# Attention with routed experts on one core: row sorting between the maxima, a first group begun on half its queries, a lead built over five groups, fills in pieces

## The chip, the cores and the metric

One core of a Trainium2 chip runs the whole program in one launch. The metric is the device time of a launch in microseconds (us). TensorE is called PE here, VectorE DVE, ScalarE ACT, GpSimd POOL, and SP is the engine that issues most DMAs.

## What is computed

The input is 4 x 1024 rows of 256, in float32. The rows are normalised; attention with 16 heads of 16 (with relative positions in a window of 4 to each side) and a mixture of 8 experts, 2 per row, both read the normalised rows, and the sum of both and the input is the output:

```python
xn = _layernorm(x, axis=-1)
x = x + _L0_attn_ref(xn, Wq, bq, Wk, bk, Wv, bv, Wo, bo, emb_rel_k, emb_rel_v) + _L0_ffn_ref(xn, gate_w, gate_b, w1, w3, w2)
# attention: softmax(q k^T + relative logits) v + relative weights x rel_v, then Wo
# experts:
logits = x @ gate_w + gate_b
top_w, top_idx = jax.lax.top_k(softmax(logits), 2)      # weights made to sum to 1
h = silu(x @ w1[e]) * (x @ w3[e]);  out = sum over the two e of (h @ w2[e]) * top_w
```

## The kernel before, in words

**Stages.** `build` runs `constants`, `norm_and_project`, `attention`, `finish_and_experts` and `combine`, each in a block of its own. A block starts when every engine has ended the one before it, so it also waits for the DMAs that SP waits for at its end.

**`norm_and_project`** takes 8 chunks of 512 rows (loop `chunks`). VectorE normalises the next chunk (L293) from `xt`, which SP loads (L200) after it has stored the one before (`put_xn`); PE projects q, k, v; ScalarE and VectorE split q and k into two float16 parts (L400, L334), which SP stores as `q_parts` and `k_parts` (L208). VectorE's L334 comes once a chunk. After chunk 3, `load_stack` (L91) issues 18 DMAs of 128 KB on SP's queue: the stacks of q and k for the first pass of groups 0 and 1 and for the second pass of group 0. All of them are waited for at the end of the block.

**`route`** (row sorting) is added to the same block after the chunks. From the gate logits VectorE finds each row's two experts, the row's place in a list sorted by expert, and the expert of each slot of 256 rows: some 60 small instructions of at most 128 x 312 elements, each waiting for the one before (L1021 to L1077). In between are one exponential on ScalarE (L1082) and two matmuls that count rows (L1088, L1089), read from PSUM by VectorE. Nine POOL instructions make its constants at the start of the block.

**`attention`** handles 16 groups of 4 heads of one batch entry. Each group has two passes. The first pass finds each query's maximum: 32 tiles of 128 queries x 1024 keys; PE makes a tile in two halves (`pass1`, L723) into one of two PSUM buffers of 1024 (`s1`), and VectorE takes its maximum (L838). Three small VectorE instructions (L842 to L845, "parts") split the 32 maxima into two float16 numbers; PE transposes them (L768), ScalarE copies them to `mt` (L904), and SP writes them as two rows into the query stack (L604), so that the second pass subtracts them in the matmul. The second pass has 64 slots: PE makes 128 keys x 512 queries (`pass2`, L733 and L737) into one of three buffers, ScalarE takes the exponential (L915), and PE sums the values (`values`, L750).

PE's order is written out in `group`: in slot n of a group's second pass it also issues first-pass matmuls of the next group, with a constant lead of 20 halves (`LEAD`); the first-pass and second-pass matmuls use different rows of the array. Group 0 has nobody ahead of it: its whole first pass runs alone, then in its own 64 slots PE issues 84 first-pass halves. The maxima of group g+1 are finished in slot 55 of group g. All of PE's instructions are in one order, so a wait in a first-pass matmul holds the second pass too.

**POOL in `attention`** makes the products of the window (32 tiles, three per group; `products` L652, `fold` L661 and L665, `add_to_band` L672, from SBUF to SBUF). Tile t waits until the parts of group t // 3 are made (`mparts_ok`). When all 32 are done it sends the rows to their slots: 64 indirect DMAs (`send`, L691), from rows loaded by `load_rows` (L677; the first two loads are issued at the start of the block).

**SP in `attention`** (`step`) writes the maxima's rows, then loads the stacks of coming groups. Between the steps it fills `slot_rows` with zeros (13 DMAs of 780 KB in steps 0 and 1) and, between steps 9 and 10, `expert_sums` with one DMA of 4224 KB (L634).

**`finish_and_experts`** runs the experts' slots; its VectorE line L1515 (two tensors from SBUF) and L1537 (one from PSUM, one from SBUF) and its POOL lines L1268 and L1270 (products from SBUF) are used by the prediction as examples. The change doesn't touch this stage.

Of the kernel before, what the change touches and what calls it, by code (L numbers as in the profile page):

```python
# [12 lines left out]
P = 128  # L13
# [6 lines left out]
CH = 512  # L20
# [81 lines left out]
def norm_and_project(nc, c, dr, x, Wq, bq, Wk, bk, Wv, bv, rel_k, gate_w, gate_b, band, dst, meta, spare, table, iota_e, slot_expert, size, w1, w3, wsum, stacks):  # L102

    with ExitStack() as ctx:
# [34 lines left out]
        logits = sb("logits", [P, NT, X])  # L139
# [34 lines left out]
        with nc.Block() as block:  # L174
            @block.sync
            def _(sp):
# [33 lines left out]
                def chunk(n, u, b):  # L210
# [28 lines left out]
                for u in range(2):  # L239
                    sp.wait_ge(stacks["in1"][u], 16 * 2 * len(Q_PARTS))  # L240
                sp.wait_ge(stacks["in2"][0], 16 * 2 * len(Q_PARTS))
# [260 lines left out]
            route(nc, block, ctx, logits, rel_out, pT, dst, meta, spare, table, iota_e, slot_expert)  # L502


def attention(nc, c, dr, stacks, band, bmax, neg, oa, dst, meta, spare):
# [5 lines left out]
    XS = 2 * TB * HG  # L511
    FOLDS = 4
    MLEAD = 9
    LEAD = 20
    MT = (LEAD - MLEAD + 1) // 2
    X1 = TB * HG
    B1, B2, BP = 2, 3, 4
    with ExitStack() as ctx:
# [57 lines left out]

        def far_pieces(tile, half):
# [8 lines left out]

        with nc.Block() as block:
            @block.sync
            def _(sp):
# [9 lines left out]

                def maximum(g, u):  # L600

                    sp.wait_ge(mt_ok, g + 1)
                    for j in range(MROWS):
                        sp.dma_start(qs[SIDE + j:SIDE + j + 1, u].rearrange("o h (i t) -> o (h i) t", t=P),  # L604
                                     mt[j * HG * TB:(j + 1) * HG * TB, :]).then_inc(m_in, 16)
# [16 lines left out]

# [5 lines left out]
                for z in range(N_ZERO // 2, N_ZERO):  # L628
                    sp.dma_start(zeros[z], zero[:].broadcast_to([P, 6, XE])).then_inc(zero_out, 16)
                for r in range(NB - 2):  # L630
                    for v in range(4):
                        step(4 * r + 2 + v, r + 1, v, v % 2)
                sums = dr["moe"].rearrange("(n p) e -> p n e", p=P)
                sp.dma_start(sums, zero[:, :, 0:E].broadcast_to([P, NT + 1, E])).then_inc(sums_out, 16)  # L634
# [5 lines left out]
                sp.wait_ge(sums_out, 16)  # L640

            @block.gpsimd
            def _(pool):
                nc.gpsimd.memset(zero[:], 0.0).then_inc(zero_ok, 1)
# [51 lines left out]
                load_rows(0)  # L696
                load_rows(1)
                for t in range(2):
                    load_window(pool, dr, t, qw[:, t, :], kw[:, t, :], win_in[t])
                for t in range(NT):  # L700

                    pool.wait_ge(mparts_ok, t // 3 + 1)
# [4 lines left out]
                    add_to_band(t, t % 2)  # L707
                for t in range(NT):
# [5 lines left out]
            def _(pe):  # L714
                def pass1(g, u, n):

                    n, half = n // 2, n % 2
                    h, i, buf = n // TB, n % TB, n % B1
                    if half == 0:
                        if n == MT or n == 0 and isinstance(g, int) and g == 1:  # L720
                            after(pe, mt_ok, g)
                        after(pe, mx_ok, g * X1 + n - B1 + 1)
# [40 lines left out]
                def maximum_rows(g, ahead=True):  # L763

                    pe.wait_ge(mparts_ok, g + 1)
                    if ahead:
                        pe.wait_ge(mx_ok, (g + 1) * X1 + MT - 1)
# [951 lines left out]
```

## Time and profile before

| | us |
|---|---|
| median of 3 runs | 1891.03 |
| lowest and highest | 1886.86 and 1902.19 |
| the profiled execution | 1900.86 |
| its span, first to last instruction | 1899.1 |
| PE / VectorE / ScalarE / POOL busy | 1699.1 / 1451.0 / 1097.8 / 811.7 |
| mean granted clock of PE (1 is 2.4 GHz) | 0.926 |

The stages of the profiled execution: the projection to 187.6, the row sorting to 207.0, group 0's first pass to 250.1, the 16 groups' second passes to 1031, the experts to some 1850, and the output. Durations in the rows are those of this one execution; busy time can hide waits inside an engine's pipeline, so the rows of waits and the starts of instructions are read beside it.

### The profile page before, as it was taken

What the parts mean: (1) busy time and instruction counts of PE and PEld (TensorE: products, weight loads), DVE (VectorE), ACT (ScalarE), POOL (GpSimd) and SP (SyncE); (2) the same over time, 40 slices, a digit from 0 to 9 for tenths busy, and PEclk for the clock granted to TensorE, in tenths of its full rate; (3) what the DMA queues carried; (4) which work ended last, traced back from release to release, by engine and by line L of the source; (5) the groups of instructions that cost most, each with busy time, mean ns of one, the idle gap of its engine ahead of it and who ended that gap; (6) DMA issues with size and microseconds to landing.
All of it is one profiled execution on the core that took longest, in us unless ns stands there. A gap on an engine that the chain in (4) does not pass through costs nothing. (4 is left out here: it accounts for less than half of the span.)

```text
span 1899.1 us, 35153 instructions
## 1 busy us (share of the span) xinstructions
PE 1699.1 (89%) x13691; PEld 1021.4 (54%) x13691; DVE 1451.0 (76%) x2569; ACT 1097.8 (58%) x2122; POOL 811.7 (43%) x587
## 2 busy tenths in 40 slices
PE   5968589999999997689996799999999999999991
PEld 3746023333333331223332687888788878888881
DVE  4535988988888984378852798999899989997652
ACT  3646047888888884368884544554455445545540
POOL 3000077778888886600000344544454445442110
PEclk9988579999999997689995899999999999999996
DMA  5999246975556655523102777777777777765745
GB/s 177 372 305 359 103 106 178 249 201 129 129 143 150 150 139 189 160 47 59 30 2 87 248 237 228 233 254 234 231 231 253 235 231 230 253 210 180 210 137 185
DMA packets 199846, 355.25 MB, mean 187 GB/s; under 512 B 17008, under 2 KB 145920, under 8 KB 191488
## 3 DMA queue, kind: packets, MB, share of 16 engines
q1 hardware_dynamic: 163360, 225.19, 40.6%
q0 software_dynamic: 27744, 106.84, 18.6%
q10 hardware_dynamic: 8576, 20.97, 3.0%
q8 instruction: 108, 1.77, 0.4%
q14 instruction: 58, 0.48, 0.1%
HBM read 281.47 MB, written 71.22 MB: 186 GB/s over the span
## 5 line engine op out<-in xcount | busy, mean ns | idle before, releaser
L838 DVE CUSTOM_DVE_ANT_0 t_seen<-t_s,hide 128x1024 bf16<-128x1024 f32 x512 | 608.4, 1222 | 135.1 <-PE t_s L723 105.8
L915 ACT ACTIVATE t_pr<-t_s 128x512 f32<-128x512 f32 x1024 | 558.8, 603 | 177.2 <-PE t_s L737 105.5
L723 PE MATMUL t_s<-ks,qs 48*128 48x512 f16 x1024 | 372.5, 414 | 36.2 <-PEq L174 12.6
L733 PE MATMUL t_s<-qs,ks 50*128 50x512 f16 x1024 | 363.7, 400 | 31.0 <-issue 17.6
L1444 ACT ACTIVATE e_sg<-e_pa,e_down 128x256 f32<-128x256 f32 x312 | 148.0, 474 | 396.9 <-PE e_pa L1319 387.5
L750 PE MATMUL t_po<-t_pr,t_vx 128*32 128x256 f32 x4096 | 344.7, 410 | 0.0
L1515 DVE SCALAR_TENSOR_TENSOR e_wl<-e_ws,e_up,e_wh 128x512 f16<-128x512 f32 x312 | 318.6, 1033 | 13.3
L1328 PE MATMUL e_py<-e_w2s,e_hT 128*128 128x256 f32 x1248 | 322.9, 381 | 0.0
L1256 POOL DMA_INDIRECT expert_sums<-e_y,e_token x78 | 139.7, 1791 | 294.0 <-DMA expert_sums<-e_y,e_token 205.0
L1319 PE MATMUL e_pa<-e_xh,e_wh 128*128 128x256 f16 x1248 | 239.8, 274 | 25.6 <-DVE e_xl L1507 18.6
L733 PEld LDWEIGHTS t_s<-qs,ks 50*128 50x128 f16 x1024 | 89.1, 94 | 285.6 <-ACT t_pr L915 173.9
L1319 PE MATMUL e_pa<-e_xl,e_wh 128*128 128x256 f16 x1248 | 239.2, 274 | 0.0
L1319 PE MATMUL e_pa<-e_xh,e_wl 128*128 128x256 f16 x1248 | 239.1, 273 | 0.0
L1328 PEld LDWEIGHTS e_py<-e_w2s,e_hT 128*128 128x128 f32 x1248 | 212.8, 190 | 22.0
L1537 DVE SCALAR_TENSOR_TENSOR e_hT<-e_pa,e_down,e_sg 128x256 f32<-128x256 f32 x312 | 145.8, 467 | 94.9 <-ACT e_sg L1444 94.9
L1405 ACT ACTIVATE e_wh<-e_ws,e_up 128x512 f16<-128x512 f32 x312 | 217.4, 711 | 0.0
L652 POOL TENSOR_TENSOR t_kw<-t_kw,t_qw 128x2304 f32<-128x2304 f32 x32 | 162.8, 5088 | 99.6 <-issue 62.2
L1319 PEld LDWEIGHTS e_pa<-e_xh,e_wh 128*128 128x128 f16 x1248 | 117.2, 98 | 83.4 <-DVE e_xl L1507 31.4
L661 POOL TENSOR_TENSOR t_kw<-t_kw 128x1152 f32<-128x1152 f32 (+2 forms) x96 | 149.9, 1562 | 7.5
L737 PEld LDWEIGHTS t_s<-far,eye 64*128 64x128 bf16 x1152 | 108.6, 98 | 69.5 <-issue 13.0
L737 PE MATMUL t_s<-far,eye 64*128 64x72 bf16 (+2 forms) x1152 | 141.6, 194 | 0.0
L723 PEld LDWEIGHTS t_s<-ks,qs 48*128 48x128 f16 x1024 | 84.6, 95 | 102.9 <-DVE t_mx L838 73.6
(231 smaller groups left out, 1936.4 us busy)
## 6 DMA issues: line engine op xcount, KB each, us to landing
e_ws<-in_L_ffn_w_dram SPq DMA_DIRECT2D x78, 1024.0 KB, 5.0
e_w2s<-in_L_ffn_w_dram SPq DMA_DIRECT2D x39, 1024.0 KB
t_kw<-k_rows POOLq DMA_DIRECT2D x32, 1152.0 KB, 8.9
e_vs<-v_rows POOLq DMA_DIRECT2D x32, 1152.0 KB, 6.0
a_wone<-in_L_ffn_w_dram ACTq DMA_DIRECT2D x16, 1024.0 KB, 10.3
qs<-q_parts SPq DMA_DIRECT2D x96, 128.0 KB, 4.0
ks<-k_parts SPq DMA_DIRECT2D x96, 128.0 KB, 6.4
slot_rows<-t_zero SPq DMA_DIRECT2D x13, 780.0 KB, 14.6
```

What stands on the lines that cost most here:

```text
L652: nc.gpsimd.tensor_tensor(held, held, qw[:, u:u + 1, :].broadcast_to([P, NM, E]), ALU.mult).then_inc(mul_ok, 1)
L661: nc.gpsimd.tensor_tensor(terms[:, :, 0:w], terms[:, :, 0:w], terms[:, :, w:2 * w], ALU.add).then_inc(fold_ok, 1)
L723: last = nc.tensor.matmul(s1[:, buf, half * CH:(half + 1) * CH], qs[lows, u, h, i * P:(i + 1) * P], ks[lows, u, h, half * CH:(half + 1) * ...
L733: last = nc.tensor.matmul(s2[:, bank, :], ks[highs, u, h, i * P:(i + 1) * P], qs[highs, u, h, half * CH:(half + 1) * CH], start=True, stop ...
L737: last = nc.tensor.matmul(s2[:, bank, a:a + m], c["eye"][SIDE:P, r, :], c["far"][SIDE:P, r, j:j + m], start=False, stop=(x == len(far) - 1 ...
L750: last = nc.tensor.matmul(po[h * VW:(h + 1) * VW, cols], vx[:, u, i, h * VW:(h + 1) * VW], pr[:, k % BP, h, cols], start=(i == 0 and part ...
L838: nc.vector.tensor_tensor_reduce(out=seen[:, buf, :], in0=s1[:, buf, :], in1=c["hide"][:, (TB - 1 - i) * P:(TB - 1 - i) * P + L], scale=1. ...
L915: nc.scalar.activation(pr[:, k % BP, n % HG], s2[:, turn(u, n)], ACT.Exp, scale=SPREAD ** -2).then_inc(exp_ok, 1)
L1319: last = nc.tensor.matmul(pa[:, f % PA, j, :], w[:, u, j, k, f * P:(f + 1) * P], x[:, u, k, :], start=(i == 0), stop=(i == len(parts) - 1))
L1328: last = nc.tensor.matmul(py[:, i, 0:E], hT[:, f, i * P:(i + 1) * P], w2s[:, u, f, :], start=(f == 0), stop=(f == FC - 1))
L1405: nc.scalar.activation(wh[:, u, m, k, cols], ws[:, m, k, cols], ACT.Copy, scale=up[:, m, bass.ds(s, 1)]).then_inc(wh_ok, 1)
L1515: nc.vector.scalar_tensor_tensor(out=wl[:, u, m, k, cols], in0=ws[:, m, k, cols], scalar=up[:, m, bass.ds(s, 1)], in1=wh[:, u, m, k, cols] ...
```

## The change

Five edits.

- **Row sorting** becomes a class `Route`. Its POOL constants are made at the start of the attention block. VectorE's instructions are yielded one by one by a generator; `maxima` takes the next one after maxima 1, 5, 9, ..., 29 of each group from 1 on (`ROUTE_EVERY`), so 8 per group and 61 places (some left empty) in groups 1 to 8. The exponential stands behind slot 56 of group 1 on ScalarE, the two counts are made by PE with the transpose of group 3's maxima, and ScalarE copies them to SBUF. The order and shapes of the instructions stay. POOL's two first `load_rows` come after the products, behind a wait for the sorted places.
- **First group.** PE makes 18 tiles of group 0 (now in an order that takes the first 4 query tiles of every head first), then half of the maxima go to the stack: 8 small DMAs in place of 2; the second pass starts on the first half of the queries. The other 14 tiles come in slots 0 to 21, their maxima follow at slot 22 by another 8 DMAs, and PE waits for them at slot 32. Group 1's first pass comes in slots 22 to 58.
- **Lead.** The lead of the first pass is 12 halves in group 1, then 14, 16, 18 and 20; the last groups are as before. ScalarE's `mt` copy and the buffers of the transposes follow from the lead.
- **Stack loads.** After chunk 6 only 6 loads are issued (first pass of group 0); the other 12 come first on SP's queue in the attention block.
- **Fills.** `expert_sums` is filled by 7 DMAs of up to 640 KB, one after each of steps 2 to 8.

The diff, cut to its core:

```diff
-                    if n == 3:
+                    if n == NC - 2:
                         for p in range(PARTS):
                             sp.wait_ge(st_part[p], 16 * 2 * KC * 2)
                         load_stack(sp, dr, stacks, 0, 0, 0, stacks["in1"])
-                        load_stack(sp, dr, stacks, 0, 0, STACK, stacks["in2"])
-                        load_stack(sp, dr, stacks, 1, 1, 0, stacks["in1"])
...
-            route(nc, block, ctx, logits, rel_out, pT, dst, meta, spare, table, iota_e, slot_expert)
+class Route:
...
+    def choose(self, dve):
...
+            self.steps += 1
+            ins.then_inc(self.chain, 1)
...
+            then(nc.vector.tensor_tensor(self.eq[:], src[:], over_x(m[:, k, :]), ALU.is_equal))
+            yield
...
-    LEAD = 20
-    MT = (LEAD - MLEAD + 1) // 2
-    X1 = TB * HG
+    LEADS = [36 - XS] + [min(12 + 2 * (g - 1), 20) for g in range(1, NG)]
+    TURN0, TURN1 = 22, 59
+    HALF = X1 // 2
+    FIRST_ROWS = 2 * MROWS * HG
+    GATES_AT, COUNT_AT = 1, 3
+    ROUTE_EVERY = 4
+    SUMS = 5
...
+        def first_passed(g, n):
+
+            if g == 0 and n < TURN0:
+                return XS + LEADS[0] + -(-(2 - LEADS[0]) * (n + 1) // TURN0)
+            if g == 0:
+                return XS + 2 + min(-(-XS * (n + 1 - TURN0) // (TURN1 - TURN0)),
+                                    XS + max(0, -(-(LEADS[1] - 2) * (n + 1 - TURN1) // (XS - TURN1))))
+            more = LEADS[min(g + 1, NG - 1)]
+            return min(NG * XS, XS * (g + 1) + LEADS[g] + -(-(XS + more - LEADS[g]) * (n + 1) // XS))
...
+                def half_maximum(u, half):
+
+                    sp.wait_ge(mt_ok, half + 1)
+                    for j in range(MROWS):
+                        for h in range(HG):
+                            row = (j * HG + h) * TB + half * CT
+                            sp.dma_start(qs[SIDE + j:SIDE + j + 1, u, h, half * CH:(half + 1) * CH].rearrange("o (i t) -> o i t", t=P),
+                                         mt[row:row + CT, :]).then_inc(m_in, 16)
...
+                load_stack(sp, dr, stacks, 0, 0, STACK, in2)
+                load_stack(sp, dr, stacks, 1, 1, 0, in1)
                 load_values(0, 0, 0)
-                maximum(0, 0)
+                half_maximum(0, 0)
                 load2(1, 0, 1, 1)
...
                 load1(2, 0)
-
+                half_maximum(0, 1)
                 step(0, 0, 2, 0)
...
-                sp.dma_start(sums, zero[:, :, 0:E].broadcast_to([P, NT + 1, E])).then_inc(sums_out, 16)
+                        piece = slice((4 * r + v) * SUMS, min((4 * r + v + 1) * SUMS, NT + 1))
+                        if piece.start < NT + 1:
+                            sp.dma_start(sums[:, piece], zero[:, :, 0:E].broadcast_to(
+                                [P, piece.stop - piece.start, E])).then_inc(sums_out, 16)
...
-                load_rows(0)
-                load_rows(1)
...
-                    pool.wait_ge(mparts_ok, t // 3 + 1)
+                    pool.wait_ge(mparts_ok, t // 3 + 2)
...
+                pool.wait_ge(route.dst_ok, 1)
+                load_rows(0)
+                load_rows(1)
...
                     for n in range(X1):
...
+                        if g == 0 and n == HALF - 1:
+                            dve.wait_ge(mx_ok, HALF)
+                            parts(slice(0, CT), 0)
+                        if g and n % ROUTE_EVERY == 1:
+                            after(dve, route.chain, route.steps)
+                            next(routing, None)
```

## Rows read from the trace of the kernel before

**Rows 1.** windows by stage: engine columns are busy us (instructions), then clock, DMA share, GB/s.
```profile
187.60:207.00 19.40, 0.58 (x2) 0.14 (x2) 17.00 (x56) 0.23 (x1) 0.01 (x1) 0.50 0.22 76
309.64:699.30 389.66, 386.24 (x4187) 140.62 (x4185) 347.33 (x604) 326.17 (x621) 318.18 (x215) 1.00 0.66 167
699.30:846.96 147.66, 110.08 (x933) 34.73 (x930) 78.41 (x135) 73.25 (x138) 76.55 (x82) 0.76 0.48 138
```

**Rows 2.** timeline of VectorE and of SP in chunks 4 to 6 (start, us, instruction).
```profile
112.58 2.48 DVE L334 SCALAR_TENSOR_TENSOR a_part<-a_qkT,size,a_part 128x1024 f16<-128x1024 f32 x2 [3.17 <-DMA k_parts<-a_part]
...
136.25 1.08 DVE L277 BATCH_NORM_STATS2 a_st<-a_xt 128x6 f32<-128x256 f32 x3 [19.79 <-DMA a_xt<-_attn_hidden_states_dram]
...
146.13 2.48 DVE L334 SCALAR_TENSOR_TENSOR a_part<-a_qkT,size,a_part 128x1024 f16<-128x1024 f32 x2 [1.82 <-DMA k_parts<-a_part]
...
164.23 2.47 DVE L334 SCALAR_TENSOR_TENSOR a_part<-a_qkT,size,a_part 128x1024 f16<-128x1024 f32 x2
...
114.37 0.51 SPq L200 DMA_DIRECT2D a_xt<-_attn_hidden_states_dram  x1
```

**Rows 3.** start of the attention block, and a window of the DMA engines before it.
```profile
192.00:194.00 2.00, 0.13 (x1) 0.14 (x2) 1.68 (x6) 0.14 (x1) 0.00 (x0) 0.50 0.01 3
...
207.00 0.37 SPq L594 DMA_DIRECT2D t_vx<-vx_rows  x1
```

**Rows 4.** timeline around the first second pass, and a window of group 0.
```profile
208.20 1.22 DVE L838 CUSTOM_DVE_ANT_0 t_seen<-t_s,hide 128x1024 bf16<-128x1024 f32 x1 [1.01 <-PE t_s L723]
...
246.01 0.18 DVE L842 TENSOR_SCALAR t_mparts<-t_mx 128x32 f16<-128x32 f32 x1
...
247.33 1.26 SPq L604 DMA_DIRECT2D qs<-t_mt  x2
...
250.09 0.58 PE L733 MATMUL t_s<-qs,ks 50*128 50x512 f16 x1 [3.08 <-DMA qs<-t_mt]
...
250.06:275.40 25.34, 24.25 (x181) 7.82 (x181) 21.37 (x35) 14.79 (x26) 23.93 (x17) 0.69 0.83 182
```

**Rows 5.** fill and scatter: the issue on SP, and windows.
```profile
705.19 0.58 SPq L634 DMA_DIRECT2D expert_sums<-t_zero  x1
...
715.00:720.00 5.00, 2.26 (x19) 0.56 (x19) 0.43 (x2) 1.06 (x2) 2.35 (x3) 0.62 1.07 393
720.00:725.00 5.00, 4.99 (x30) 0.87 (x26) 3.16 (x6) 2.71 (x6) 0.98 (x2) 0.50 0.75 271
800.00:805.00 5.00, 1.53 (x11) 0.21 (x3) 1.15 (x1) 1.19 (x2) 3.89 (x4) 0.66 0.32 110
```

**Rows 6.** who PE waited for in groups 1 to 9 (total us, times, longest).
```profile
PE t_s L723 <- DVE t_mx L838: 1.7, 9, 0.2
```

**Rows 7.** timeline of VectorE and POOL in the expert stage, and the page's row of L1515.
```profile
1059.82 0.75 DVE L1515 SCALAR_TENSOR_TENSOR e_wl<-e_ws,e_up,e_wh 128x512 f16<-128x512 f32 x1
...
1061.12 4.11 POOL L1270 TENSOR_TENSOR e_prod<-e_vs,e_e 128x2304 f32<-128x2304 f32 x1
...
1061.71 0.48 DVE L1537 SCALAR_TENSOR_TENSOR e_hT<-e_pa,e_down,e_sg 128x256 f32<-128x256 f32 x1 [1.14 <-ACT e_sg L1444]
...
1062.32 3.47 DVE L1515 SCALAR_TENSOR_TENSOR e_wl<-e_ws,e_up,e_wh 128x512 f16<-128x512 f32 x1
...
L1515 DVE SCALAR_TENSOR_TENSOR e_wl<-e_ws,e_up,e_wh 128x512 f16<-128x512 f32 x312 | 318.6, 1033 | 13.3
```

**Rows 8.** POOL's round in a group, and the start of the next group's.
```profile
468.78 5.09 POOL L652 TENSOR_TENSOR t_kw<-t_kw,t_qw 128x2304 f32<-128x2304 f32 x1 [5.76 <-issue]
473.95 4.83 POOL L661 TENSOR_TENSOR t_kw<-t_kw 128x1152 f32<-128x1152 f32 x3
...
512.08 5.09 POOL L652 TENSOR_TENSOR t_kw<-t_kw,t_qw 128x2304 f32<-128x2304 f32 x1 [5.74 <-issue]
```

**Rows 9.** two forms of the row sorting, one shape (busy us, mean ns | idle).
```profile
L1050 DVE TENSOR_TENSOR r_scan<-r_scan 128x128 f32<-128x128 f32 x1 | 0.3, 293 | 0.0
...
L1049 DVE COPY r_scan<-r_scan 128x128 f32<-128x128 f32 x1 | 0.2, 226 | 0.0
```

More of the change, by code:

```diff
@@ L238, in _ @@
                     sp.wait_ge(st_part[p], 16 * 2 * KC * NC)
[L239 to L241 removed]
+                sp.wait_ge(stacks["in1"][0], 16 * 2 * len(Q_PARTS))
             @block.gpsimd
@@ L714, in _, with pass1 @@
             def _(pe):
-                def pass1(g, u, n):
-                    n, half = n // 2, n % 2
-                    h, i, buf = n // TB, n % TB, n % B1
+                def pass1(at):
+                    tile, half = at // 2, at % 2
+                    g, u, buf = tile // X1, tile // X1 % 2, tile % B1
+                    h, i = tile_of(tile % X1)
                     if half == 0:
-                        if n == MT or n == 0 and isinstance(g, int) and g == 1:
-                            after(pe, mt_ok, g)
-                        after(pe, mx_ok, g * X1 + n - B1 + 1)
+                        if tile % X1 == 0:
+                            pe.wait_ge(in1[u], 16 * N_STACK * (g // 2 + 1))
+                        for behind in (g - 1, g):
+                            if behind >= 0 and tile == rows_tile(behind):
+                                pe.wait_ge(mt_ok, behind + 2)
+                        after(pe, mx_ok, tile - B1 + 1)
                     last = nc.tensor.matmul(s1[:, buf, half * CH:(half + 1) * CH], qs[lows, u, h, i * P:(i + 1) * P],
@@ new lines, in maximum_rows @@
+                def maximum_rows(g):
+                    tile = rows_tile(g)
+                    buf = tile % B1
+                    pe.wait_ge(mparts_ok, g + 2)
+                    pe.wait_ge(mx_ok, tile - B1 + 1)
+                    last = nc.tensor.transpose(s1[:, buf, 0:P // 2].bitcast(F16), mparts[:].rearrange("p j h i -> p (j h i)"),
+                                               c["ident16"][:])
+                    if g == COUNT_AT:
+                        last = route.count(pe, s1[:, buf, P:P + NT * X], s1[:, buf, CH:CH + NT * X])
+                    last.then_inc(mt_ps_ok, 1)
@@ L835, in maxima @@
                     for n in range(X1):
-                        h, i, buf = n // TB, n % TB, n % B1
+                        buf = n % B1
+                        h, row = tile_of(n)
                         dve.wait_ge(s1_ok, g * X1 + n + 1)
                         nc.vector.tensor_tensor_reduce(
-                            out=seen[:, buf, :], in0=s1[:, buf, :], in1=c["hide"][:, (TB - 1 - i) * P:(TB - 1 - i) * P + L],
-                            scale=1.0, scalar=LOW, op0=ALU.add, op1=ALU.max, accum_out=mx[:, h, i:i + 1]).then_inc(mx_ok, 1)
@@ L841, in maxima @@
-                    dve.wait_ge(mx_ok, (g + 1) * X1)
-                    link(nc.vector.tensor_scalar(mparts[:, 0], mx[:], -1.0 / ONE, None, ALU.mult), 1)
-                    link(nc.vector.scalar_tensor_tensor(out=mparts[:, 1], in0=mx[:], scalar=-1.0 / ONE, in1=mparts[:, 0],
-                                                        op0=ALU.mult, op1=ALU.subtract), 2)
-                    nc.vector.tensor_tensor(neg_v[:, b, v], mparts[:, 0], mparts[:, 1], ALU.add).then_inc(mparts_ok, 1)
+                            out=seen[:, buf, :], in0=s1[:, buf, :], in1=c["hide"][:, (TB - 1 - row) * P:(TB - 1 - row) * P + L],
@@ new lines, in maxima @@
+                            scale=1.0, scalar=LOW, op0=ALU.add, op1=ALU.max, accum_out=mx[:, h, row:row + 1]).then_inc(mx_ok, 1)
+                        if g == 0 and n == HALF - 1:
[4 more added lines that the diff above has]
+                            next(routing, None)
+                    dve.wait_ge(mx_ok, (g + 1) * X1)
@@ L847, in _ @@
+                    if g == 0:
+                        dve.wait_ge(mt_ps_ok, 1)
+                        parts(slice(CT, TB), 1)
+                    else:
+                        parts(slice(0, TB), g + 1)
                 nc.vector.memset(mparts[:], 0.0).then_inc(zeros_ok, 1)
```

414 lines of the change are left out of this document (234 added, 180 removed).

## The prediction

> **What bounds the kernel now.** I read the page first (TensorE, PE, busy 89% of the span; VectorE, DVE, 76%), then its clock line, for the stretches in which PE is slow, then the windows of those stretches, which say which engine ends what [rows 1]. From 309.64 to 699.30, nine groups of attention, PE is busy for 386.24 of 389.66 us at full clock, 43.30 us a group; VectorE has 347.33 us and ScalarE 326.17 us. A microsecond that PE waits there is lost, since nothing later has slack to give it back. The kernel waits in four places instead: in the projection, in the 19.40 us of row sorting in which only VectorE works, in the 43 us of group 0's maxima, and in groups 10 and 11 (147.66 us against 86.60).
>
> **The sum's base.** The profiled execution took 1900.86 us (span 1899.1), 9.8 above the median 1891.03. I sum against 1900.9 and take 9.8 off at the end.
>
> **The stack loads that leave the projection.** The second-part subtraction on VectorE comes once per chunk. It starts 18.1 us apart in chunks 5 and 6 (146.13 to 164.23), but 33.55 between chunks 4 and 5 (112.58 to 146.13), where VectorE sat idle 19.79 us for the input load of chunk 5 [rows 2]. That load stood in SP's queue behind the 18 stack loads, was issued at 114.37 and landed 21.9 us later. After the change no load of x is behind them: 6 loads come after chunk 6, whose next chunk was loaded earlier. Gain 33.55 - 18.1 = 15.4 us; ends 12 (part of the wait was other traffic) and 19.8 (the whole wait). The 6 remaining loads stand ahead of chunk 7's stores, when the DMA engines are busy all the time; a third as many loads should hold them up for at most a third of 19.79, 0 to 7 us; I take 3.5.
>
> **Row sorting out of the gap.** The sorting keeps VectorE alone at work for 17.00 of 19.40 us [rows 1], and the next block starts at 207.00. Without it the block would wait for SP's last stores: the DMA engines are idle from 192 on (share 0.01), so with the last wait and the start the block would begin near 193.3 [rows 3]. Gain 13.7 us (13 to 15). The POOL constants that now lead the new block are nine small instructions ahead of window loads whose products wait 40 us for maxima: nothing. The two row loads moved behind the products only delay the scatter, whose cover is groups 12 to 15: nothing.
>
> **Group 0 on half its queries.** Let T be the block's start. The maxima come each 1.18 us (208.20 to 246.01, 32 of them), so half of them end at T+20.1; parts, transpose and copy took 1.3 us (246.01 to 247.33); two row DMAs took 1.26 us to issue and 1.5 to land, eight take 5.0 and 1.5. The second pass starts at T+28 against T+43.1 [rows 4]. But VectorE, which then has 18 tiles behind it and 51.5 to go until group 1 begins, idles some 5 us meanwhile and sets the rest: 22 slots at the low clock at the rate of 250.06 to 275.40, 23.5 us; then 37 slots with 32 tiles, 37.8 us plus parts 0.7, the sorting's own eight instructions 3.2 and the wait at the transpose 1.3; then 5.5 us for 3.5 tiles and the maxima's way into the queries. Group 1 starts at T+100 against 309.64 - 207.0 = T+102.6. Gain 2.6 us; ends -8 (the second eight DMAs stand behind 13 loads on SP and PE waits for them at slot 32) and +8. So the earlier start is mostly given back. The lead then grows from 12 to 20, two more first-pass matmuls in each of four groups: at most 8 x 0.39 = 3 us, mostly beside second-pass ones; I take 1.2.
>
> **Fill in pieces.** The single 4.2 MB fill is issued at 705.19, as the scatter starts; the DMA engines are full until 720 (share 1.07), PE is busy 2.26 of 5 us, and the clock falls to its lower level, 0.50 through 725 [rows 5]. But the two groups lose 61 us in all, much of it late: from 800 to 805 PE is busy 1.53 of 5 us at a DMA share of 0.32, with the fill long over. So the scatter alone does it too. I take 3 us (-5 to +9). Seven pieces among loads that leave a third of the DMA time free cost nothing.
>
> **Sorting between the maxima: the largest term.** 61 places come after maxima 1, 5, ..., 29 of groups 1 to 8. The instructions' own time is small: mean 0.3 us. After each group's three parts instructions (0.65 us on VectorE) PE waited 0.2 us, 9 times in nine groups [rows 6]. So alone they would cost 0 to 3 us, and I would take 1.5.
>
> But where they stood before, POOL was idle. Now POOL runs its products, and in the expert stage the trace shows what this does. L1515, which reads two tensors from SBUF, started 1.2 us into POOL's 4.11 us product and took 3.47 us, to 0.56 after that product's end; alone it takes 0.75. L1537, started in the same product, reads PSUM and one tensor from SBUF, and took its normal 0.48. The mean of its 312 is 1.033, so 88 us are above 0.75, 2.8 for each of POOL's 32 products [rows 7]. So a VectorE instruction with two SBUF tensors is held until POOL's is over. The maxima, which read PSUM and one tensor from SBUF, run beside POOL in every group at their 1.22 us [rows 4] and aren't.
>
> POOL's round in a group begins 0.1 us after the group's parts and is fixed: 5.09, then 4.83 in three pieces (2.6, 1.4, 0.7), two short ones; again after 12.55 us and a third time, then idle until the next parts, 43.30 us later [rows 8]. The places lie at 2.8, 8.2, 13.6, 19.0, 24.5, 29.9, 35.3 and 40.7 us after the parts (four tiles of 1.353 apart), and each hold moves those behind it. A held instruction waits 2.4 us at 2.8, 1.2 at 8.2, 4.1 at 13.6, 1.7 at 28.6, 0.4 at 29.9. The code's order gives 27 instructions with two SBUF tensors. Stepped through, groups 1 to 8 are held for 4.1, 4.5, 0.4, 0.5, 3.2, 5.9, 5.8 and 2.4 us, 26.8 in all. With two first-pass buffers PE needs a tile's maximum about 0.5 us after it comes now; it waits the rest at the next first-pass matmul, with second pass, values and ScalarE behind it in order. The instruction's own 0.4 us uses up that slack, so the holds cost PE their whole 26.8 us.
>
> 19 more are copies and scalar operations from SBUF to SBUF. No row shows one beside POOL. Like the one-input L1537 they could run free (0); held as the others are, the same stepping gives 44.6 us, 17 more. Of 128 elements a copy takes 226 ns, the two-input form 293 [rows 9]: the copy is the faster by 67 ns, as if it moved its elements by two paths, perhaps with the one that L1515 waited for. I take half, 8.5.
>
> The Trainium skill ("SBUF — State Buffer", Who interferes with whom) states that a VectorE instruction with two SBUF inputs, or in a mode that uses both ports (copies and scalar operations can be), and a GpSimd instruction that reads SBUF take turns whole. The trace agrees for the first kind; no row here shows the second. By the page the whole 17 us would be paid and the forecast would be 1913.
>
> PE waits of 3 to 4 us in a group also cost clock: in and after PE's hole of 715 to 720 it was granted 0.62 and then 0.50, some 8 us at 1.2 of its 2.4 GHz [rows 5]. In 250.06 to 275.40, at a clock of 0.69, a slot took 1.1 us [rows 4] against 43.30 / 64 = 0.677, so a drop costs about 3 us. I take it in about three of eight groups, 8 us (0 to 24).
>
> ScalarE's exponential of the gap, at slot 56 of group 1, comes some 10 slots after VectorE's step for it; the counts add two ScalarE copies and two matmuls once. Both under 1 us, inside the bounds.
>
> **Sum.** -15.4 + 3.5 - 13.7 - 2.6 + 1.2 - 3.0 = -30.0; +26.8 + 8.5 + 8.0 = +43.3. Net +13.3: 1914.2 by the profiled execution, 1904.4 by the median. Forecast 1904, its own range 1890 to 1922.
>
> **Rivals.** A, the holds cost nothing: VectorE's holds fall where PE has tiles enough or POOL gives way, only the instructions' own 1.5 us remain. For it: VectorE idles 42 us in nine groups, about as much as the holds. Against it: two buffers hold 2.7 us of tiles, a hold of 4 can't be spread, and L1515 was held each time. 1900.9 - 30.0 + 1.5 - 9.8 = 1862.6: faster. B, slower still: copies are held too and each group's largest hold (2.4 to 4.6 us) drops the clock: 26.8 + 17 + 24 = 67.8, less 30 gives 1929; it decides from the point where one hold is over about 3 us. C, the change doesn't free the projection: the six loads stall chunk 7 as the 18 stalled chunk 5, the 15.4 go, and the holds are as small as in A: 1878.
>
> **How the numbers follow.** Forecast 0.52, A 0.30, B 0.12, C 0.06. Within 1% of 1891 (1872 to 1910, about what a measurement tells from no change) lie C and 0.31 of the forecast's 0.52; the rest of it, 0.21, and B are slower. So faster 0.30, same 0.37, slower 0.33. The likeliest case is a no-change that hides two large terms. The range must reach to A and nearly to B: 1858 to 1932.
>
> **What would show it.** In the profile after: chunk pitches of the subtraction all near 18 us; the attention block starting near 180 instead of 207; group 1 starting about 28 us earlier. Sorting instructions with two SBUF tensors lasting 1 to 4 us instead of 0.42, and groups 1 to 7 at 45 to 50 us apart instead of 43.30 (by POOL's first product in each), with PE waits for maxima of 2 to 4 us. If they last 0.2 to 0.5 us and the groups stay at 43.3 to 43.6, the largest term is wrong and A is right. If copies last over 0.3 us, the half I took should be whole. If the groups 10 and 11 lose far less than 50 us, the fill was underrated.

## The result and the profile after

The changed kernel takes **1955.16 us** (median of 4 runs, 1941.96 to 1969.47), the kernel before 1895.8 beside it: ratio 1.0315, 95% interval 1.0269 to 1.0361. Slower by 3%, where I forecast 1904 and gave 1932 as the upper end. The profiled execution after took 1969.47 us, span 1967.8. Some executions of a kernel are over 1.5% longer than its fastest; the ratios leave them out, and the profile of the reduction in experiment 7 is one of them, with its groups at the same 43.30 us.

The windows of both kernels' stages after the projection (window, us; engine columns busy us; clock, DMA share, GB/s), cut where groups begin (to within 1.3 us: the cuts before lie at a group's first exponential, those after just ahead of it, at 298.85 for group 1 and 758.25 for group 10). Before, group 0 and group 15 (the groups between: [rows 1]):

```profile
208.20:309.64 101.44, 87.17 (x534) 21.64 (x533) 88.94 (x153) 36.91 (x68) 54.04 (x41) 0.68 0.40 110
...
975.73:1026.20 50.47, 49.27 (x393) 16.16 (x395) 10.84 (x5) 36.21 (x68) 0.00 (x0) 0.77 0.00 1
```

After: group 0, groups 1 to 9, groups 10 and 11, group 15:

```profile
181.16:297.60 116.44, 93.50 (x520) 22.65 (x518) 93.09 (x155) 38.72 (x70) 45.48 (x37) 0.57 0.41 97
297.60:757.30 459.70, 419.75 (x4200) 147.12 (x4196) 401.37 (x659) 328.36 (x623) 325.63 (x222) 0.92 0.58 152
757.30:900.50 143.20, 108.07 (x934) 35.11 (x937) 78.52 (x134) 73.16 (x138) 79.03 (x86) 0.80 0.43 119
1029.30:1094.50 65.20, 64.83 (x404) 18.26 (x404) 11.76 (x5) 37.40 (x70) 0.00 (x0) 0.55 0.00 1
```

Read the second row against the one of before for the same nine groups [rows 1]: PE's work is the same, its busy time 33 us longer at a clock of 0.92 and not 1.00, and the wall time 70 us longer: the other 36.5 us are time in which PE idles. The two spans split in this way; the third column is a second profiled execution of the changed kernel, on another chip (below):

| | before | after | after, again |
|---|---|---|---|
| start to the first maximum | 208.20 | 181.16 | 187.35 |
| first maximum to group 1 | 101.44 | 116.44 | 108.64 |
| groups 1 to 9 | 389.70 | 459.70 | 463.01 |
| groups 10 and 11 | 147.62 | 143.20 | 86.70 |
| groups 12 to 14 | 128.77 | 128.80 | 128.76 |
| group 15 to the end | 923.4 | 938.5 | 913.6 |

So 27.0 us are gained ahead of the attention and 4.4 in groups 10 and 11; 15.0 are lost in group 0, 70.0 in groups 1 to 9 and 15.1 behind: +68.7. The last is in this execution alone: group 15 ran at 0.55 here, and took 41.42 us at full clock in the second one. With every cut at the first exponential group 0 loses 16.3, groups 1 to 9 lose 69.7 and group 15 loses 14.1; no reading below hangs on the difference.

The projection is freed of its stall: the block starts at 179.97 (the first load on SP), and the subtraction L329 begins at 112.10 and 130.81, 18.7 us apart, where 33.55 stood before [rows 2, 3]. Timelines of VectorE and SP after:

```profile
112.10 2.48 DVE L329 SCALAR_TENSOR_TENSOR a_part<-a_qkT,size,a_part 128x1024 f16<-128x1024 f32 x2 [3.31 <-DMA k_parts<-a_part]
...
130.81 2.48 DVE L329 SCALAR_TENSOR_TENSOR a_part<-a_qkT,size,a_part 128x1024 f16<-128x1024 f32 x2 [5.15 <-DMA k_parts<-a_part]
```
```profile
179.97 1.26 SPq L91 DMA_DIRECT2D qs<-q_parts  x3
```

And the sorting between the maxima is held. The first instruction of it (VectorE, after), and GpSimd's product:

```profile
232.68 2.98 DVE L599 TENSOR_SCALAR r_iota_k<-r_iota_i 128x16 f32<-128x16 int32 x1
235.57 1.21 DVE L1084 CUSTOM_DVE_ANT_0 t_seen<-t_s,hide 128x1024 bf16<-128x1024 f32 x1
...
418.11 4.65 DVE L646 COPY r_scan<-r_scan 128x8 f32<-128x8 f32 x1
```
```profile
230.57 5.05 POOL L886 TENSOR_TENSOR t_kw<-t_kw,t_qw 128x2304 f32<-128x2304 f32 x1 [45.24 <-DVE neg L1079]
```

A scalar operation with one input, on 16 elements, waits for the product's end at 235.62, and the next maximum behind it. A copy of 8 elements took 4.65 us. The 55 sorting instructions last 64.9 us in all, and of the 48 us above their unheld time (measured below) 22 are the 27 with two SBUF inputs, 26 the 19 copies, casts and scalar operations; the 8 reductions and the one reciprocal add nothing. The first pass of a group is made while the group before it has its second, so in time nine of the 55 lie in group 0 and the others in groups 1 to 7. PE's waits in groups 1 to 9 (us, times, longest), where before had 1.7, 9, 0.2 [rows 6]:

```profile
PE t_s L962 <- DVE t_mx L1084: 32.5, 29, 4.3
PE t_s L972 <- DMA qs<-t_mt: 3.8, 1, 3.8
```

### The profile page after: what moved, and what is told of

Same layout as the page of the kernel before. It is cut to its first block and busy times, and to the rows that moved or that the text cites. A ratio compares the mean times of both kernels' runs of the same rounds, so it can differ in the third digit from the quotient of the medians.

```text
span 1967.8 us, 35245 instructions
## 1 busy us (share of the span) xinstructions
PE 1750.4 (89%) x13692; PEld 1029.0 (52%) x13692; DVE 1493.6 (76%) x2571; ACT 1101.0 (56%) x2125; POOL 810.9 (41%) x587
## 5 line engine op out<-in xcount | busy, mean ns | idle before, releaser
L962 PE MATMUL t_s<-ks,qs 48*128 48x512 f16 x1024 | 386.1, 433 | 66.0 <-DVE t_mx L1084 48.3
L972 PE MATMUL t_s<-qs,ks 50*128 50x512 f16 x1024 | 390.0, 426 | 40.5 <-issue 18.0
L989 PE MATMUL t_po<-t_pr,t_vx 128*32 128x256 f32 x4096 | 372.9, 440 | 0.0
L1629 DVE SCALAR_TENSOR_TENSOR e_wl<-e_ws,e_up,e_wh 128x512 f16<-128x512 f32 x312 | 318.9, 1034 | 13.3
L976 PEld LDWEIGHTS t_s<-far,eye 64*128 64x128 bf16 x1152 | 113.8, 103 | 77.1 <-issue 28.3
L976 PE MATMUL t_s<-far,eye 64*128 64x72 bf16 (+2 forms) x1152 | 147.8, 201 | 0.0
## 6 DMA issues: line engine op xcount, KB each, us to landing
slot_rows<-t_zero SPq DMA_DIRECT2D x13, 780.0 KB, 14.1
```

The source lines that it names most:

```text
L962: last = nc.tensor.matmul(s1[:, buf, half * CH:(half + 1) * CH], qs[lows, u, h, i * P:(i + 1) * P], ks[lows, u, h, half * CH:(half + 1) * ...
L972: last = nc.tensor.matmul(s2[:, bank, :], ks[highs, u, h, i * P:(i + 1) * P], qs[highs, u, h, half * CH:(half + 1) * CH], start=True, stop ...
L976: last = nc.tensor.matmul(s2[:, bank, a:a + m], c["eye"][SIDE:P, r, :], c["far"][SIDE:P, r, j:j + m], start=False, stop=(x == len(far) - 1 ...
L989: last = nc.tensor.matmul(po[h * VW:(h + 1) * VW, cols], vx[:, u, i, h * VW:(h + 1) * VW], pr[:, k % BP, h, cols], start=(i == 0 and part ...
L1629: nc.vector.scalar_tensor_tensor(out=wl[:, u, m, k, cols], in0=ws[:, m, k, cols], scalar=up[:, m, bass.ds(s, 1)], in1=wh[:, u, m, k, cols] ...
```

## The experiments

Four chips were used, and the kernel before took 1899, 1839, 1843 and 1892 us on them. Nearly the whole difference lies in groups 10 and 11 (last section), so kernels are compared by their ratio to before on the same chip, and by the lengths of their groups, which agree between chips elsewhere.

**1. The sorting in one piece at the start.** `choose` is run to its end before the first maximum, with the counts' matmuls and copies and the exponential there too.

```
-                        if g and n % ROUTE_EVERY == 1:
-                            after(dve, route.chain, route.steps)
-                            next(routing, None)
+                while True:
+                    after(dve, route.chain, route.steps)
+                    if next(routing, 0) == 0:
+                        break
```

> The kernel after with the whole row sorting put back into one piece: VectorE does it before the first maximum of the attention, while GpSimd has no products; everything else of the change stays. Theory H (sorting instructions between the maxima are held by GpSimd's products, TensorE waits for the late maximum, and the granted clock falls behind it): groups 1 to 8 go from a mean of 53 us back to 43.3 each, about 70 us less; group 0 gets part of its lost clock back (up to 15 us less); the piece at the start costs 14 us; so about 1870 to 1895 us. Rival L (the new lead and the new order of the first pass's tiles slow the groups, whatever the sorting does): still 1940 to 1965 us, and groups 1 to 8 at over 50 us. Rival C (the extra time is the clock of this chip at random): groups 1 to 8 differ from run to run, with no sorting in them some still above 48 us.

1899.1 us, ratio 0.9981 (0.9931 to 1.0030). The windows of the first maximum to group 1, of groups 1 to 4 and of groups 5 to 9:

```profile
207.13:312.69 105.56, 89.45 (x522) 22.56 (x522) 83.27 (x147) 37.67 (x69) 42.47 (x26) 0.61 0.25 62
312.69:492.25 179.56, 171.54 (x1871) 62.26 (x1872) 159.81 (x279) 145.44 (x277) 148.23 (x104) 1.00 0.78 203
492.25:708.75 216.50, 214.60 (x2327) 78.14 (x2325) 193.03 (x336) 181.18 (x346) 177.93 (x119) 1.00 0.61 155
```

Groups 5 to 9 take 43.30 us each again, at full clock: the spread sorting costs 459.7 - 396.1 = 63.6 us in groups 1 to 9 (33.6 of them more busy time of PE for the same matmuls, 30.0 idle time), and 3 to 11 in group 0 (10.9 here, of which 4.1 busy). What stays is not nothing: groups 1 to 4, where the lead grows, are 6.4 us too long, and the way to group 1 is 4.1 us longer than before. The time is 4 us above the expected range since the piece costs 20 us at the block's start (first maximum 21.6 us behind the first load) and not 14. Rival L is left with these 10.5 us of the loss; rival C is out.

**2. The products left out.**

```
-                    products(t, t % 2, t // 2)
-                    fold(t, t % 2)
+                    pool.wait_ge(win_in[t % 2], 32 * (t // 2 + 1))
+                    nc.gpsimd.tensor_copy(dot[:, t % 2, 0:1], qw[:, t % 2, 0:1]).then_inc(band_ok, 1)
```

> The kernel after with the sorting left where the change puts it, between the maxima, and GpSimd's products of queries and window keys and their folding left out (the band then holds only its first part; the window loads and all waits stay). Theory H (held by the products): no sorting instruction takes over 1.2 us, the sum of the sorting is 17 us or less in place of 60, groups 1 to 9 take 43.3 us, and up to 45.5 where the lead is still built (first run: 45.5, 44.5, 44.5, 45.0 with the sorting gone); the time is 1955 - 64 - 11 = about 1880 us. Rival O (the sorting costs its own time and the waits of its chain, whoever else runs): over 1930 us, with groups 1 to 8 over 50 us.

This kernel leaves out the products, so its output is not the attention's; only its times are used. Ratio 1.0267 (1.0191 to 1.0342): the time I expected did not come, the durations did. The 55 instructions last 16.4 us in all, the longest 0.48. Windows of 64 slots in groups 3, 5 and 7, and what PE waited for in the second:

```profile
401.08:447.31 46.23, 43.26 (x471) 15.67 (x474) 41.08 (x76) 36.28 (x69) 3.75 (x9) 1.00 0.61 152
493.11:545.31 52.20, 44.93 (x469) 16.24 (x472) 39.46 (x75) 36.64 (x69) 3.74 (x9) 0.90 0.49 129
598.92:642.22 43.30, 42.92 (x469) 15.81 (x473) 38.79 (x70) 36.23 (x69) 3.75 (x9) 1.00 0.63 163
```
```profile
PE t_s L972 <- DMA qs<-t_mt: 6.6, 1, 6.6
PE t_s L962 <- DVE t_mx L1084: 0.5, 2, 0.4
```

The window in group 3 has seven of the sorting instructions in it and takes 46.23 us at full clock, with 1.3 us of waits for maxima; the one in group 7 has three and takes 43.30. The window in group 5, with eight, is long for another reason: PE waits 6.6 us for the rows of maxima. Over groups 1 to 9 such waits come to 25.3 us, 8 times, and those for maxima to 7.3. Without products GpSimd issues the window loads of three tiles at once (the last at 487.39), just ahead of the rows (SP, 487.83). That these loads are what delays the rows is read from that order, and no run tests it. The experiment removed a stall and made one. It shows who holds the instructions, not the price.

**3. The sorting in groups 0 and 1, the products one group later.**

```
-                        if g and n % ROUTE_EVERY == 1:
+                        if n >= 16 or g:
...
-                    pool.wait_ge(mparts_ok, t // 3 + 2)
+                    pool.wait_ge(mparts_ok, t // 3 + 3)
```

> The kernel after with the sorting, one step behind each maximum from the 17th of group 0 to the end of group 1, and GpSimd's products begun one group later, so that the two don't meet. Theory H: groups 1 to 8 back to 43.3 us each, group 0 not longer than in the kernel before (T+100), about 1865 to 1885 us, faster than both kernels. Rival O (VectorE has no room for the steps' own 17 us): 17 to 30 us more than that, about 1895 us. Rival L: over 1930 us.

1913.2 us, ratio 1.0094 (1.0042 to 1.0146). I had counted the places wrong: of the 61, 48 come before the products' start at 287.80 and 13 behind it. VectorE on both sides of it, and GpSimd:

```profile
286.94 0.16 DVE L666 TENSOR_TENSOR r_start<-r_ends,r_slots 128x8 f32<-128x8 f32 x1
...
288.76 4.12 DVE L668 TENSOR_SCALAR r_start<-r_start 128x8 f32<-128x8 f32 x1
...
300.49 5.19 DVE L677 TENSOR_TENSOR r_pick<-r_hot,r_place 128x256 f32<-128x256 f32 x1
```
```profile
287.80 5.04 POOL L886 TENSOR_TENSOR t_kw<-t_kw,t_qw 128x2304 f32<-128x2304 f32 x1 [96.59 <-DVE neg L1079]
...
300.36 5.04 POOL L886 TENSOR_TENSOR t_kw<-t_kw,t_qw 128x2304 f32<-128x2304 f32 x1
```

Every sorting instruction before 287.80 took 0.15 to 0.42 us, five behind it 1.6 to 5.2: the two above end at 292.88 and 305.68, the products at 292.84 and 305.40. Two of the five fall at the end of group 0, three in group 1, and from the first maximum to the end of group 1 it took 173 us, 22 more than in experiment 1. So the time missed theory H's range by 28 us. Against theory H: from group 4 on the groups take 44.00 and not 43.30, with no sorting in them. I have no cause for that.

**4. The same eight steps a group, in the last four tiles.** There GpSimd is done with its round [rows 8].

```
-                        if g and n % ROUTE_EVERY == 1:
-                            after(dve, route.chain, route.steps)
-                            next(routing, None)
+                        if g and n >= X1 - 4:
+                            for _ in range(2):
+                                after(dve, route.chain, route.steps)
+                                next(routing, None)
```

> The kernel after with the same eight steps of the sorting to a group, but two behind each of the group's last four maxima in place of one behind every fourth: there GpSimd has done its three tiles and waits 5.8 us for the next group. Theory H: nearly no instruction held; two steps of 0.2 to 0.5 us behind each other cost TensorE up to 2 us in a group, so groups 1 to 8 at 44 to 47 us, about 1890 to 1910 us. Rival O (steps cost their own time and chain wherever they stand, two together more than one): groups 1 to 8 at over 50 us, 1940 us or more.

Ratio 1.0019 (0.9973 to 1.0066), 3% better than the change, whose ratio was 1.03 on both chips on which it ran. The copy that took 4.65 us, in its new place:

```profile
416.74 0.17 DVE L646 COPY r_scan<-r_scan 128x8 f32<-128x8 f32 x1
416.94 0.42 DVE L648 TENSOR_TENSOR r_scan<-r_scan 128x248 f32<-128x248 f32 x1
```

No instruction is above 0.48 us; their sum is 16.5. But groups 1 to 8 took 378.8 us and not 352.8 as in experiment 1: pairs of steps make PE wait 0.9 us at a time at most, 11.1 in all, and behind three of the eight blocks of steps the clock still fell to 0.50. Ahead of two of these falls PE had three waits for maxima of 1.7 us together (453 to 466) and four of 2.3 (550 to 562).

**5 to 7. One instruction a group.** The kernel before, with one unused instruction behind the first maximum of groups 1 to 9, while GpSimd's product runs: the addition below, a copy of 128x8, or a maximum over 128x256. Two of the nine fall in group 0's second pass, seven in those of groups 1 to 7.

```
+                        if n == 0 and 0 < g < 10:
+                            dve.wait_ge(d_ok, g)
+                            nc.vector.tensor_tensor(d_out[:], d_in[:, 0], d_in[:, 1], ALU.add).then_inc(d_ok, 1)
```

> The kernel before with one instruction more on VectorE in each of groups 1 to 9, behind the group's first maximum, where GpSimd has just begun a product of 5.1 us: an addition of two SBUF tiles of 128x256 into a third (nothing uses it). It measures what one held instruction costs a group that otherwise takes 43.30 us. Theory H: the instruction takes 3 to 4 us in place of 0.42, TensorE waits 2 to 3 us for the next maximum, the granted clock may fall behind that wait, and the group takes 46 to 52 us: 25 to 75 us over the nine. Rival O (no hold; its own 0.42 us): 43.3 to 43.7, under 4 us over the nine.

> As the run with one addition, but a copy of 128x8 (one SBUF input, eight elements to a partition), which takes 0.17 us by itself. The forecast counted half of such instructions as held. Theory H2 (a copy is held just as an addition is): as the addition, 3 to 4 us and 46 to 52 us a group. Rival (one input is not held): 0.17 us and 43.3 us a group, as before.

> As the run with one addition, but a maximum over 128x256 into 128x32 (the form of L602), which took 0.41 us in every place in the trace of after. Theory H: never held, 0.41 us, 43.3 to 43.7 us a group, within 4 us of before. Rival (any instruction put between maxima there costs as much, since TensorE waits for the next maximum and its clock falls): 45 us or more a group.

Ratios 1.0397 (1.0342 to 1.0452), 1.0306 (1.0232 to 1.0381) and 0.9959 (0.9907 to 1.0012). The instruction in each (ns: least, median, most):

```profile
L845 DVE TENSOR_TENSOR t_d_out<-t_d_in x9: 2309/4437/4439, 249.9 to 667.2; 128x256 f32<-128x256 f32 x9
```
```profile
L845 DVE COPY t_d_out<-t_d_in x9: 2071/4180/4189, 255.7 to 661.7; 128x8 f32<-128x8 f32 x9
```
```profile
L845 DVE TENSOR_REDUCE t_d_out<-t_d_in x9: 414/416/418, 250.5 to 599.7; 128x32 f32<-128x256 f32 x9
```

The reduction costs nothing: groups 1 to 9 take 389.71 us. Each of the others is held 4.0 us (median), and its group takes 9.3 us more with the addition ((368.00 - 7 x 43.30) / 7), 8.6 with the copy; single groups take from 5.6 to 15.0 more. The windows behind one addition, held from 355.64 to 360.08 (three us each):

```profile
355.00:358.00 3.00, 2.81 (x30) 1.04 (x28) 3.00 (x3) 1.72 (x4) 3.00 (x1) 1.00 0.00 0
358.00:361.00 3.00, 0.07 (x3) 0.00 (x0) 3.00 (x2) 0.60 (x1) 2.92 (x2) 0.92 0.00 0
361.00:364.00 3.00, 2.72 (x21) 0.84 (x25) 2.58 (x6) 0.60 (x1) 2.91 (x2) 0.50 0.02 5
364.00:367.00 3.00, 3.00 (x24) 0.85 (x24) 1.23 (x2) 1.74 (x3) 2.54 (x5) 0.50 0.12 20
```

PE uses up its two buffers, waits 3.21 us for the maximum that the addition delays, and its granted clock goes to 0.50 (1.2 GHz) just when it has work again; it stays there for some 6 us. Of the 9.3 us 3.9 are idle time of PE (3.4 the waits for maxima), and 5.4 more busy time for the same 3257 matmuls, at a clock of 0.88 over the seven groups and not 1.00. Nine small instructions cost some 77 us (64.9 in groups 1 to 7, 11.7 in group 0 against the run with the reduction), as much as all of the sorting does in the changed kernel. This is theory H with its price.

**8. The kernel before with its stack loads moved, nothing else.**

```
-                    if n == 3:
+                    if n == NC - 2:
...
-                        load_stack(sp, dr, stacks, 0, 0, STACK, stacks["in2"])
-                        load_stack(sp, dr, stacks, 1, 1, 0, stacks["in1"])
```

> The kernel before with one part of the change alone: of the three stack loads inside the projection one is left, placed behind the last chunk but one, and the other two stand at the head of the attention. Forecast's first term: the subtraction's long pitches go, 15.4 us less, 3.5 us given back by the load that moves; about 1884 us (1880 to 1888). Rival P (the two loads at the attention's head delay its first second pass or first passes): the projection is 15 us shorter and the time within 5 us of 1896.

1885.3 us, ratio 0.9934 (0.9893 to 0.9975). The first maximum comes at 191.40, 16.8 us earlier than before, and group 1 starts 102.21 us behind it (101.44 before). The time moved by 12.5 (4.7 to 20.3) where the term was 11.9. Rival P is out.

**9. The same with the fill in pieces.**

> The kernel before with two parts of the change: the stack loads out of the projection (measured at 1885 us alone) and the fill of the sums in seven pieces in place of one. Forecast's term of the pieces: -3 us (-5 to +9), about 1882 us; groups 10 and 11 together 143.5 to 145 us in place of 147.6. Theory with the pieces worthless: 1885 us, groups 10 and 11 at 147.6. Either way this would be the fastest kernel so far.

Ratio 0.9973 (0.9932 to 1.0015): not to be told from experiment 8, nor from before. The test decides nothing on the pieces, since this chip has no loss in groups 10 and 11 to win back: 86.80 us with the pieces, and 86.70 in experiment 10. Nor is it the pieces that take the loss away: the kernels of experiments 5 and 7 keep the one fill, and on their chip the two groups took 86.60 and 86.65. On the two chips with the loss, the stretch took 147.6 and 147.8 us with one fill (before, experiment 8) and 143.1 to 146.8 with pieces (after and experiments 1, 3 and 12; in experiment 3 it is groups 11 and 12, since the products end a group later). That agrees with my 3 us, one execution each.

**10. The changed kernel again.**

> The kernel after, unchanged, beside the kernel before on this chip. What the runs so far say: on the chips used, the kernel before takes 1896, 1899 or 1839 us, so only ratios and groups are compared. Ratio 1.03 again. Two things of the first trace are tested: group 15 took 65.2 us at a clock of 0.50 where the kernel before took 50.5; if that was chance it comes out at 41 to 52 us here; if it is the change's, at 65 again. Groups 1 to 9 at 459 us in the first trace: theory H says 445 to 475 again; if the clock's fall is chance, anything.

Ratio 1.0326 (1.0261 to 1.0392); its spans are the third column of the table. Groups 1 to 9 lose 73 us again, so the clock's falls are no chance; group 15's was.

**11. All 32 tiles of group 0's first pass ahead, on top of experiment 1.**

```
-    LEADS = [36 - XS] + [min(12 + 2 * (g - 1), 20) for g in range(1, NG)]
+    LEADS = [0] + [min(12 + 2 * (g - 1), 20) for g in range(1, NG)]
```

> The kernel of the first run (sorting in one piece at the start) with group 0 opened as in the kernel before: TensorE does all 32 tiles of its first pass ahead of the second pass, not 18. It tests the forecast's term of the opening on half the queries alone. Forecast: 2.6 us slower than the first run's 1899, about 1902. Rival (the traces of the first run give group 1 at T+127.1 less 20.5 of sorting = T+106.6 against T+102.6 before, so the half opening costs): about 4 us faster than the first run, 1895.

Ratio 1.0094 (1.0038 to 1.0150) against 0.9981: slower, so neither expectation's number held. From the first maximum to group 1 it took 122.13 us, experiment 1 105.56, before 101.44. This kernel keeps the new turn structure, in which 22 turns bring next to no first pass and the 37 behind them 32 tiles; from 291 to 327, in the second part, the clock was 0.50. The half opening is worth 17 us within the new structure, but the structure as a whole is 4 us worse than the old.

**12. The lead built at once, on top of experiment 1.**

```
-    LEADS = [36 - XS] + [min(12 + 2 * (g - 1), 20) for g in range(1, NG)]
+    LEADS = [36 - XS] + [20 for g in range(1, NG)]
```

> The kernel of the first run (sorting in one piece at the start, ratio 0.998 to before) with the first pass's lead of 20 half tiles built wholly in group 0, as in the kernel before, in place of over five groups. It tests the forecast's term of the lead (+1.2 us). In the first run groups 1 to 4 took 45.5, 44.5, 44.5 and 45.0 us, 6.3 us over four times 43.3. If the lead only moves work, those four go back to 43.3 each and group 0 grows by 5 to 8 us: ratio unchanged within 0.3%. If building it over five groups costs by itself, group 0 grows by under 3 us and the ratio falls to 0.995. If group 0, which runs at a granted clock of 0.6, pays double for each tile, it grows by over 10 us and the ratio rises to 1.002 or more.

Ratio 1.0018 (0.9984 to 1.0052), which experiment 1's interval overlaps. Way to group 1, group 1 and group 2:

```profile
200.05:304.81 104.76, 88.15 (x522) 21.89 (x522) 83.16 (x147) 37.39 (x69) 41.32 (x26) 0.61 0.26 65
304.81:355.54 50.73, 48.14 (x476) 16.60 (x477) 44.12 (x78) 36.60 (x70) 42.68 (x32) 0.93 0.83 220
355.54:398.83 43.29, 42.91 (x467) 15.64 (x465) 38.59 (x68) 36.23 (x69) 35.52 (x25) 1.00 1.00 273
```

Groups from 2 on take 43.3, group 0 is as long as in experiment 1, and group 1 takes the 7.4 us that groups 1 to 4 shared there. But the edit doesn't do what I expected of it. `first_passed` caps group 0 at the pace of its turns, so in both kernels 140 first-pass halves come ahead of group 1 (the kernel before has 150). The other ten come at once in group 1's first turn, 5.3 us from one second-pass matmul to the next, and the clock is 0.50 behind them. So building the lead in one burst costs about as much as over four groups; what it would cost inside group 0 no run shows. The opening with the lead is 10.5 us longer than before's in experiment 1 (4.1 + 6.4) and 10.7 here (3.3 + 7.4).

## Why the prediction was wrong

The sum said +13.3 us for the profiled execution, it was +68.7. By its steps:

- **Loads and sorting out of the front**, -25.6: -27.0, and -20.9 in the second execution. Right, to within the 12 us by which the block's start moves between executions (last section), and the loads alone by experiment 8.
- **Group 0 on half its queries and the lead**, -1.4 together: +10.5. The second pass did start at T+28 (207.93 against 179.97), but what I gave back later was too little: in experiment 1 turns 22 to 58, with 32 tiles of first pass in them, took 49.9 us at a clock of 0.62 (258.12 to 308.06), where the sum had 37.8 + 0.7 + 1.3 = 39.8 without the sorting, and each tile of lead that group 0 doesn't do costs a later group 1.3 us (6.4 for five), not 0.3. Inside the bounds of -8 and +8 for the one, outside of 3 for the other.
- **Fill in pieces**, -3: -4.4. It agrees, by one execution each.
- **Sorting between the maxima**, +43.3: this is the step that failed, by size and not by kind, and within it above all the clock. It cost 63.6 us in groups 1 to 9 and 10.9 in group 0 (116.44 - 105.56; 3.1 in the second execution), 74.5: 37.7 in busy time of PE for the same matmuls, 36.8 in idle time. The holds of the two-input instructions came to 22.0 where I stepped out 26.8. Of the **one-input copies and scalar operations "I take half, 8.5"**: they were held as fully as the others, 26.4 us. The Trainium skill ("SBUF — State Buffer", Who interferes with whom) says so of copies, casts and scalar operations in a two-port mode and exempts reductions; the runs agree on each: the added copy 4.2 us, the cast L688 1.6, the scalar operation L599 3.0, the reduction 0.4. It would have put my forecast at 1913, still under the range's 1932. What is wrong too is that "the holds cost PE their whole" length: 48.4 us of holds (64.9 - 16.5) left PE idle for 36.8, against 26.8 + 8.5 = 35.3 in the sum. That these two agree is luck, an error in the copies against one in the overlap.
- **The clock**, "in about three of eight groups, 8 us (0 to 24)": 33.6 us of more busy time in groups 1 to 9 and 4.1 in group 0, 37.7. Busy time can hide short waits, so the split is not sharp, but it says the same as experiment 5, where a hold of 4.0 us cost a group 3.9 in idle and 5.4 in busy time. I took it that only a wait of 3 to 4 us drops the clock. In experiment 4 it dropped twice behind waits for maxima of at most 0.9 us each. Group 0, which I left out of this term, is where the first hold stands (232.68): the clock was 1.00 from 228 to 234 and 0.50 from 240 to 280. In experiment 2, with no hold, it was still 1.00 from 238 to 252, and 0.50 only from 262 on.
- **Chance**: group 15 took 15 us more in this one execution. The median is 14 us lower than this execution.

Rival B had the mechanism (copies held too, each largest hold drops the clock) and 1929, still 26 us short of the median; I gave it 0.12. Rival A was out at once. The sign of the forecast, no change at all, came from halving the two costs that I could not see, while the gains stood in rows.

The one part worth keeping is the first: experiment 8 beats both kernels, by 0.7% (0.3 to 1.1) and, by the ratios, 3.7%; experiment 9, the same with the pieces on a chip without the loss, has 0.3% and an interval that reaches over 1.

## What to carry to other kernels

Before work moves from a gap into a full stage, ask of each instruction which engine shares its way to SBUF there: beside GpSimd's long products only reductions, one reciprocal (0.35 us, with the product running for 1.1 more) and instructions with a PSUM input ran free; additions, copies, casts and scalar operations of any size waited for the product's end. If they must go there, put them where GpSimd waits. Don't price a stall of TensorE in a stage that it bounds by its length (here 3.9 us of idle time cost 9.3), but by a kernel with one stalled instruction a group.

## What the runs showed of the hardware

- **A hold's length is the other's rest, not its own size.** A copy of 8 elements took 4.18 us, an addition of 256 took 4.44; both end with the product, to within 0.3 us. Even a cast of one partition (L688, 0.17 us alone) took 1.61 in experiment 3.
- **Chips differ in one stretch.** Groups 10 and 11 with the scatter took 147.8 us on one chip and 86.8 on another, at full clock, with all other groups alike. GpSimd's 64 scatters lasted 976 ns each on both. What PE waited for in those two groups, in experiment 8 and in experiment 9 (us, times, longest):

```profile
PE t_s L731 <- issue: 25.1, 13, 5.5
PE t_s L731 <- ACT t_pr L913: 4.4, 4, 1.7
```
```profile
PE t_s L726 <- DVE t_mx L841: 0.8, 3, 0.4
```

  The 25.1 us are waits for nothing that the profile shows, and beside its waits PE was busy for 25 us longer in experiment 8 (111.16 and 85.83), at a clock of 0.76. The scatter and the one fill stand in kernels with the loss and in kernels without it, so neither makes the 61 us by itself, as I had put it; what does stays open. Two of the four chips of the experiments had it, and so had the first two profiles.
- **The projection's end moves.** With the same code ahead of it, the block's first load was issued between 177.62 and 189.26 in eight executions (after and experiments 1 to 4 and 10 to 12), and both ends are of one chip; a single profile can't settle a term of that size.
- **Equal groups, another length.** 44.00 us a group in experiment 3, at full clock and with the same instructions in the stretch, is not explained.
